# The experts' weights in a ring of eight, down weights on 96 rows, slot rows asked for on ScalarE's queue

## The reference

```python
slot = flat * C + jnp.minimum(pos, C - 1)          # C = 96 slots for each of E = 64 experts
buf = jnp.zeros((E * C, H), x.dtype).at[slot].set(x[tok]).reshape(E, C, H)
g = jnp.einsum('ech,emh->ecm', buf, Wg)            # H = 256, M = 176
u = jnp.einsum('ech,emh->ecm', buf, Wu)
out = jnp.einsum('ecm,ehm->ech', jax.nn.silu(g) * u, Wd).reshape(E * C, H)
y = jnp.sum(out[slot].reshape(T, K, H) * topk_w[..., None], axis=1)
```

## Time and profile before

| | |
|---|---|
| median of 3 runs | 1161.46 us (1160.77 to 1165.43) |
| the profiled execution | 1160.57 us |
| its span | 1158.8 us |
| TensorE busy | 1036.8 us (89%) |
| attention and shared expert | up to some 910 us |
| experts | some 910 to 1130 us |
| combine | some 1130 us to the end |

### The profile page before, as it was taken

The page is one execution under the profiler, slowest core; times in us unless marked ns, Lnnn a source line. Parts: engine busy times, 40 slices in busy tenths (PEclk is TensorE's granted clock), DMA queues, the critical chain, the costliest instruction groups (busy, mean ns, idle before and its releaser), DMA issues.

```text
span 1158.8 us, 18069 instructions
## 1 busy us (share of the span) xinstructions
PE 1036.8 (89%) x5813; PEld 859.1 (74%) x5813; DVE 613.2 (53%) x1429; ACT 493.5 (43%) x905; POOL 416.7 (36%) x601
## 2 busy tenths in 40 slices
PE   4999999999999999999999999996879887777774
PEld 4689898899989889988888899895545554444443
DVE  3674546566586567578565856853374211111116
ACT  1355555455545455554544565454220222333320
POOL 2232224432225643222763322374026143444440
PEclk9999999999999999999999999998899999999995
DMA  9960000001001100100110000002010598889866
GB/s 364 340 210 0 0 0 1 1 1 38 1 1 53 71 18 1 37 1 1 68 43 8 19 19 1 1 19 83 10 55 5 134 233 211 224 224 234 227 131 217
DMA packets 59189, 95.74 MB, mean 83 GB/s; under 512 B 8203, under 2 KB 41750, under 8 KB 58608
## 3 DMA queue, kind: packets, MB, share of 16 engines
q1 hardware_dynamic: 46880, 80.66, 21.7%
q0 software_dynamic: 12240, 14.16, 6.4%
HBM read 62.17 MB, written 42.15 MB: 90 GB/s over the span
## 4 chain that ended last, share of the span: by engine, by line
PE 72%; DMA 12%; DVE 9%; issue 3%; POOL 1%; ACT 1%; SPq 0%; DVEq 0%; POOLq 0%; ACTq 0%
PE ps L1145 21%; PE ps L1168 11%; PE ps L1192 11%; DMA wds<-in_wd 9%; PE ps L1181 9%; PE ps L1357 4%; PE ps L1229 3%; PE ps L1372 3%; PE ps L1154 2%; PE ps L1175 2%; PE ps L1157 2%; DVE arena L866 2%; PE ps L1304 2%; DMA acc<-wos,arena 1%; PE ps L1126 1%
## 5 line engine op out<-in xcount | busy, mean ns | idle before, releaser
L392 POOL TENSOR_TENSOR holdp<-neghalf 128x1 f32<-128x1 f32 x139 | 30.1, 216 | 508.7 <-DVE ss L760 267.8
L541 ACT ACTIVATE prob<-ps,rn 128x512 f32<-128x512 f32 (+3 forms) x256 | 121.1, 526 | 178.4 <-PE ps L1168 178.3
L1145 PE MATMUL ps<-wh,hth 128*128 128x384 f32 x512 | 177.8, 347 | 8.5 <-DVE wl L714 4.6
L760 DVE TENSOR_REDUCE ss<-arena 128x8 f32<-128x1024 f32 x64 | 78.1, 1220 | 198.4 <-ACT arena L525 198.3
L1145 PE MATMUL ps<-wh,htl 128*128 128x384 f32 x512 | 172.4, 337 | 0.0
L1145 PE MATMUL ps<-wl,hth 128*128 128x384 f32 x512 | 172.3, 337 | 0.0
L1168 PE MATMUL ps<-qt,kt 128*128 128x512 f32 (+3 forms) x512 | 149.6, 435 | 11.6 <-DVE arena L779 5.8
L525 ACT ACTIVATE arena<-ps 128x1024 f32<-128x1024 f32 x64 | 65.6, 1025 | 221.4 <-PE ps L1145 221.4
L1192 PEld LDWEIGHTS ps<-vx,prob 128*128 128x128 f32 x1280 | 152.9, 191 | 4.0 <-POOL prob L439 0.8
L1192 PE MATMUL ps<-vx,prob 128*128 128x129 f32 (+1 forms) x1280 | 153.4, 274 | 0.5 <-POOL prob L439 0.5
L504 POOL DMA_INDIRECT acc<-wos,arena x64 | 90.2, 1409 | 142.4 <-ACT wos L649 105.0
(11 more groups left out here) (165 smaller groups left out, 1605.1 us busy)
## 6 DMA issues: line engine op xcount, KB each, us to landing
wgus<-in_wgu SPq DMA_DIRECT2D x64, 352.0 KB
wds<-in_wd SPq DMA_DIRECT2D x64, 176.0 KB
slot_rows<-pay SPq DMA_DIRECT2D x1, 7728.0 KB, 35.5
arena<-slot_rows SPq DMA_DIRECT2D x64, 120.8 KB, 3.3
warena<-in_wqkv SPq DMA_DIRECT2D x1, 4992.0 KB, 20.2
acc<-zrow SPq DMA_DIRECT2D x2, 2048.0 KB, 30.1
warena<-acc SPq DMA_DIRECT2D x8, 512.0 KB, 7.5
wos<-in_wo SPq DMA_DIRECT2D x1, 2048.0 KB, 28.3
```

Source lines behind the costliest of these rows:

```text
L541: act_(prob[:, OFF[j]:OFF[j] + w], sflat[:, OFF[j]:OFF[j] + w], ACT.Tanh, scale=rn[:, bass.ds(head(n), 1), TT + j:TT + j + 1].squeeze(1)). ...
L760: nc.vector.tensor_reduce(ss[:].rearrange("p (c i) -> p i c", c=2), sq, X, ALU.add).then_inc(s["ss_rdy"], 1)
L1145: last = mm(ps[:, i, 0:3 * DH], hp[:, k, i * P:(i + 1) * P], wp[:, k, :], start=(k == 0 and m == 0), stop=(k == KC - 1 and m == 2))
```

## The change

It has three parts.

The down weights come from the host padded from 88 to 96 rows; the matmuls read the first 88 as before. The ring of weights has eight places: four own ones (`wge`, `wde`, loaded at the kernel's start as before) and four in tiles that the attention is through with (`prob`, `arena`, `vx`, `wos`), loaded by SyncE once the last head is done. Each weight load in the stage is then for expert u+8. The output rows keep four places (`ORING`). The load of the slot rows leaves SyncE's list; ScalarE asks for it behind `e_orow(f)`, for expert f+4, for f from 4 to 59. The wait for the scatter is the one that `e_orow` has anyway.

```diff
-RING = 4
+EARLY = 4
+RING = 8
+ORING = 4
 XR = 8
+MR = 96
@@ 
-        orow = wos[0:C, 0:RING, :]
+        orow = wos[0:C, 0:ORING, :]
+        late = XR * RW
...
+        wgus = [wge[:, u] for u in range(EARLY)]
+        wgus += [gu_place(prob[:, 0:2 * KC * M]), gu_place(prob[:, 2 * KC * M:4 * KC * M])]
+        wgus += [gu_place(arena2[:, late:late + 2 * KC * M]), gu_place(arena2[:, late + 2 * KC * M:late + 4 * KC * M])]
+        wds = [wde[:, u] for u in range(EARLY)]
+        wds += [wd_place(vx[0:MR, 1024:1536]), wd_place(vx[0:MR, 1536:2048]), wos[0:MR, 4:6, :], wos[0:MR, 6:8, :]]
@@ SyncE, after the attention
+            sp.wait_ge(s["o_rdy"], B * H)
+            sp.wait_ge(s["y_rdy"], B * H)
+            sp.wait_ge(s["x2_rdy"], 2 * B + 1)
+            for u in range(EARLY, RING):
+                sp.dma_start(wgus[u], wgu[u]).then_inc(w_in[u], 16)
+                sp.dma_start(wds[u], wd[u]).then_inc(w_in[u], 16)
@@ SyncE, in the experts
-            def rows_in(base, u):
-                sp.wait_ge(ys[u % NACC], (base + (u - RING + NACC - u % NACC)) * (16 // NACC))
-                sp.dma_start(xg[0:C, (u + RING) % XR, :], buf_d[bass.ds((base + (u + RING)) * C, C), :]).then_inc(xg_in[(u + RING) % XR], 16)
...
-                if not (first and u < RING) and not (last and u >= XR - RING):
-                    rows_in(base, u)
@@ ScalarE
+            def e_rows(e, base):
+
+                n = e + XR - ORING
+                a.dma_start(xg[0:C, n % XR, :], buf_d[bass.ds((base + n) * C, C), :]).then_inc(xg_in[n % XR], 16)
@@ 
                 e_silu(e, base)
                 if not (isinstance(base, int) and base + e < 2):
-                    e_orow(e - 2, base) if e >= 2 or isinstance(base, int) else e_orow(e - 2 + XR, base - XR)
+                    f, at = (e - 2, base) if e >= 2 or isinstance(base, int) else (e - 2 + XR, base - XR)
+                    e_orow(f, at)
+                    if not (isinstance(base, int) and not ORING <= base + f < E - (XR - ORING)):
+                        e_rows(f, at)
@@ the host
-        "wd": a("L0_ffn_Wd").transpose(0, 2, 1).reshape(E, 2, MC, D).transpose(0, 2, 1, 3),
+        "wd": np.pad(a("L0_ffn_Wd").transpose(0, 2, 1).reshape(E, 2, MC, D).transpose(0, 2, 1, 3), ((0, 0), (0, MR - MC), (0, 0), (0, 0))),
```

More of the change, by code:

```diff
@@ L86, in build @@
         gates = sb("gates", [P, KC, E])
-        wgus = sb("wgus", [P, RING, KC, 2 * M])
-        wds = sb("wds", [MC, RING, 2, D])
+        wge = sb("wge", [P, EARLY, KC, 2 * M])
+        wde = sb("wde", [MR, EARLY, 2, D])
         warena = sb("warena", [P, KC * H * 3 * DH])
@@ L191, in build, with gu_place, wd_place @@
         actt = xnf[0:MC, 512:512 + 4 * C].rearrange("p (u m c) -> p u m c", u=2, m=2)
-        orow = wos[0:C, 0:RING, :]
+        orow = wos[0:C, 0:ORING, :]
+        late = XR * RW
+        def gu_place(v):
+            return v.rearrange("p (k m) -> p k m", k=KC)
+        def wd_place(v):
+            return v.rearrange("p (m d) -> p m d", m=2)
+        wgus = [wge[:, u] for u in range(EARLY)]
[3 more added lines that the diff above has]
+        wds += [wd_place(vx[0:MR, 1024:1536]), wd_place(vx[0:MR, 1536:2048]), wos[0:MR, 4:6, :], wos[0:MR, 6:8, :]]
         accs = [warena[:, (a + 1) * NT * D:(a + 2) * NT * D].rearrange("p (i d) -> p i d", i=NT) for a in range(NACC)]
@@ L222, in build @@
         ys = [sem(f"ys{a}") for a in range(NACC)]
-        o95s = [sem(f"o95s{i}") for i in range(RING)]
+        o95s = [sem(f"o95s{i}") for i in range(ORING)]
         acc_in = [sem(f"acc_in{b}") for b in range(B)]
@@ L287, in _ @@
             sp.dma_start(gates[:], gate).then_inc(s["ld_gate"], 16)
-            for u in range(RING):
-                sp.dma_start(wgus[:, u], wgu[u]).then_inc(w_in[u], 16)
-                sp.dma_start(wds[:, u], wd[u]).then_inc(w_in[u], 16)
+            for u in range(EARLY):
+                sp.dma_start(wgus[u], wgu[u]).then_inc(w_in[u], 16)
+                sp.dma_start(wds[u], wd[u]).then_inc(w_in[u], 16)
             sp.wait_ge(s["fills"], 2)
@@ L337, in gate_up @@
                 sp.wait_ge(s["gu_ps"], base + (u + 1))
[L338 to L342 removed]
+                sp.dma_start(wgus[u % RING], wgu[bass.ds(base + (RING + u), 1)].squeeze(0)).then_inc(w_in[u % RING], 16)
             def last_row(base, u):
                 sp.wait_ge(s["orow_rdy"], base + (u + 1))
[L346 removed]
+                sp.dma_start(o95_d[bass.ds(base + u, 1)], orow[C - 1:C, u % ORING, :]).then_inc(o95s[u % ORING], 16)
             def down(base, u):
                 sp.wait_ge(s["dn_ps"], base + (u + 1))
[L350 removed]
+                sp.dma_start(wds[u % RING], wd[bass.ds(base + (RING + u), 1)].squeeze(0)).then_inc(w_in[u % RING], 16)
             def sp_period(base, u):
@@ L354, in sp_period @@
                 last = isinstance(base, int) and base == E - XR
-                if not (last and u >= XR - RING):
+                if not last:
                     gate_up(base, u)
                 if not (first and u < 2):
-                    if not (last and u - 2 >= XR - RING):
+                    if not last or u < 2:
                         down(base, u - 2)
                     last_row(base, u - 2)
-                if not (first and u < RING) and not (last and u >= XR - RING):
-                    rows_in(base, u)
             for u in range(XR):
@@ L372, in _ @@
             last_row(E - XR, XR - 1)
-            for u in range(RING):
-                sp.wait_ge(o95s[u], 16 * (E // RING))
+            for u in range(ORING):
+                sp.wait_ge(o95s[u], 16 * (E // ORING))
             sp.dma_start(o95, o95_d).then_inc(s["o95_ld"], 16)
@@ L504, in _ @@
                 pool.indirect_dma_start(acc_d[e % NACC], bass.IndirectOffsetOnAxis(ap=xg[0:C, e % XR, TOK:TOK + 1].bitcast(I32), axis=0),
-                                        orow[0:C, e % RING, :], None, bounds_check=NTOK - 1, oob_is_err=False,
+                                        orow[0:C, e % ORING, :], None, bounds_check=NTOK - 1, oob_is_err=False,
                                         compute_op=ALU.add).then_inc(ys[e % NACC], 16)
@@ L642, in e_orow @@
                 if isinstance(base, int):
-                    if e >= RING:
-                        a.wait_ge(ys[e % NACC], 16 * ((e - RING) // NACC + 1))
-                        a.wait_ge(o95s[e % RING], 16 * (e // RING))
-                else:
-                    a.wait_ge(ys[e % NACC], (base + e - RING + NACC - e % NACC) * (16 // NACC))
-                    a.wait_ge(o95s[e % RING], (base + e - e % RING) * (16 // RING))
-                act_(orow[:, e % RING, :], ps[0:C, 4 + e % 2, 0:D], ACT.Copy,
+                    if e >= ORING:
+                        a.wait_ge(ys[e % NACC], 16 * ((e - ORING) // NACC + 1))
+                        a.wait_ge(o95s[e % ORING], 16 * (e // ORING))
+                else:
+                    a.wait_ge(ys[e % NACC], (base + e - ORING + NACC - e % NACC) * (16 // NACC))
+                    a.wait_ge(o95s[e % ORING], (base + e - e % ORING) * (16 // ORING))
+                act_(orow[:, e % ORING, :], ps[0:C, 4 + e % 2, 0:D], ACT.Copy,
                      scale=xg[0:C, e % XR, bass.ds(D + (base + e), 1)]).then_inc(s["orow_rdy"], 1)
+            def e_rows(e, base):
+                n = e + XR - ORING
+                a.dma_start(xg[0:C, n % XR, :], buf_d[bass.ds((base + n) * C, C), :]).then_inc(xg_in[n % XR], 16)
             def e_period(e, base):
@@ L1356, in gu @@
                 for k in range(KC):
-                    last = mm(ps[0:C, 1 + e % 2, 0:2 * M], xgt[:, e % 2, k, :], wgus[:, e % RING, k, :], start=(k == 0), stop=(k == KC - 1))
+                    last = mm(ps[0:C, 1 + e % 2, 0:2 * M], xgt[:, e % 2, k, :], wgus[e % RING][:, k, :], start=(k == 0), stop=(k == KC - 1))
                 last.then_inc(s["gu_ps"], 1)
@@ L1371, in down @@
                 for m in range(2):
-                    last = mm(ps[0:C, 4 + e % 2, 0:D], actt[:, e % 2, m, :], wds[:, e % RING, m, :], start=(m == 0), stop=(m == 1))
+                    last = mm(ps[0:C, 4 + e % 2, 0:D], actt[:, e % 2, m, :], wds[e % RING][0:MC, m, :], start=(m == 0), stop=(m == 1))
                 last.then_inc(s["dn_ps"], 1)
```

## The result

The changed kernel takes 1418.65 us in the median (1416.56 to 1423.19, 4 runs), the kernel before 1163.45 us beside it: a ratio of 1.2184 with the interval 1.2145 to 1.2222. It is slower, as forecast, but by 255 us and not by 179; the range ended at 1390. The profiled execution took 1416.56 us with a span of 1414.8 us.

What follows compares the result with a forecast made beforehand. Before, late expert weights bound the kernel (48.9 us of waits). After, 55 passes of 6.65 us from 929.6 us reach 1295.4; 42.6 to the span's end and 1.8 outside give 1339.8, about 1341 us in the median; range 1268 to 1390.

Steps and rivals of the forecast that it cites:

- the prediction's closing balance: Whole kernel: 52 us gained where weights no longer wait, 231 lost in row waits and slow clock, 179 more.
- The place of the loss: Experts 8 to 63: the transpose behind down waits for slot rows with no lead, some 3 us each, about 170 us.
- The signs: Expert stage: granted clock 0.7 to 0.9, DMA share near 0.45, 7 to 8 scatters in 50 us.
- the pass of 6.65 us: Each pass of experts 8 to 63: 2.62 us TensorE work, 3.03 gap, 1.0 for the clock.
- The clock: TensorE after each idle 3.0 us: six of ten passes at the lower level, +1.0 us a pass.
- The wait: Down's end to next transpose: 0.10 to scaling, 0.30 to issue, 2.5 landing, 0.13 to matmul, 3.03 us.
- my light case: Slot-row landing where eight transfers were issued alone: 2.1 / 2.4 / 2.8 us; 2.5 taken as nearest to it.
- The upper bound: Slot-row landing from issue: at most 3.8 us, the full stage's median behind two weight transfers on SyncE's queue.
- The one with the clock at full: Expert passes: the clock holds, a pass of 5.65 us, 1286 us, band 1260 to 1310; chance 0.25.
- The one with the clock low in nearly all passes: Expert passes: low clock, 7.25 us, 1374 us, or rows landing as late as before, 1388; band 1366 to 1425; chance 0.20.
- The rival on the other side: Transpose behind down: rows not late, DMA engines bound the pass, kernel faster at 1144 us; chance 0.02.
- the queue rule: DMA engines take turns between queues, so rows on ScalarE's queue land as when light; standing in line costs 73 us.

Runs made afterwards that it cites:

- the twin with lead: Changed kernel with ScalarE asking for the slot rows two passes ahead, behind a wait for the scatter: 1138.4 us, ratio 0.9772.
- the 1.0034 above: Kernel before, ring of four and 88 rows, with ScalarE asking for the slot rows two passes ahead: 1165.79 us, ratio 1.0034.

## Why the prediction was right and wrong, point by point

**What bounds the kernel before: right in the main.** The weights' landing bounds it, and the ring takes those waits away. But it brings 17 us (0.9876), not the 49 of the list of waits and not the 52 written into the prediction's closing balance: the DMA engines then stand at 0.89 to 0.92 (950 to 1100 us), and the rows (29.3 us of waits in 30 passes) and the scatters become the next to be late. The balance took the pitch of TensorE, 2.5 us, for what is next; 2.9 is what the twin with lead reaches.

**The place of the loss: right.** The order showed the load behind down and the transpose right behind the same down. Undoing this part gives 0.9808, this part alone 1.2326.

**Cost of the other parts.** The four loads after the attention cost nothing visible: the first transpose of the stage starts at 911.74 us, before at 910.69, and two kernels without these loads start it at 909.0 and 913.8. The padding was put at 0 and is a small gain of its own, 6 to 7 us. What it does in the changed kernel, with the DMA engines at 0.40, no run shows.

**The size: wrong.** By the profiled execution the forecast was 1339.8 us and 1416.6 came. The transpose of expert 8 starts 2.7 us later than summed (932.34 for 929.6; 1.05 us of it are the later start of the stage, 1.70 a first wait of 4.73 in place of 3.03), the 55 passes take 1.30 us more each (7.95 for 6.65), 71.7 us, and the rest behind expert 63 takes 2.4 us more. The signs were missed on the same side: a granted clock of 0.64 where 0.7 to 0.9 was forecast, and 6 scatters in 50 us for 7 to 8. The step that failed is the pass of 6.65 us. Its mechanism was right and two of its terms were too small, the clock by 1.03 us and the wait by 0.27:
- *The clock*, put at +1.0, was about +2.0. The wait of 3.30 us leaves 7.95 - 3.30 = 4.65 us of work, against 2.62 + 1.0 = 3.62. The price of a slow pass was read from the pass at 958 us, where gate-up took 1.94 us; that pass was only partly at the lower level, and a whole one takes 2.55 for gate-up and 4.95 in all, 2.3 more than 2.62 and not 1.6. And by these numbers (4.65 - 2.62) / 2.33 = 0.87 of this price was paid in the mean, where I had taken six of ten passes. A slow pass does bring the clock back, but late: 28 of the 55 passes regain it before their end, only to lose it in the next wait, and gate-up pays in all of them.
- *The wait*, put at 3.03, was 3.30. The step from scaling to issue was 0.16, less than the 0.30 taken. The landing was 2.8, not 2.5: my light case was eight loads of rows with no weight load beside them, while here the two weight loads of the same pass are asked for just ahead; without them it is 2.1. The upper bound was misread too. The 3.8 us of the earlier trace rows is the landing of all transfers with `arena` in their name, and the scatters, which read it too, are among them; the slot rows alone took 2.3/3.3/4.1 us, so the full stage stretched them less than I had thought. That the DMA share is halved does not help if what is left stands at the same moment.
- The two are tied. At the full clock the rows follow the weights more closely and land after 3.5 us; the pass without any loss of clock is 6.6 us, not 5.65. A sum of 5.65 and a clock term hid this.

**The rivals.** The one with the clock at full did not come; made by hand, it gives 1331 us, not 1286. The one with the clock low in nearly all passes came, with 7.95 in place of the 7.25 that its top price gave for the clock alone. Its band, 1366 to 1425, held the time, but it had a chance of 0.20 and the range cut it at 1390. The rival on the other side did not come; its place, the transpose behind down, was the right one to look at, and with lead given back the time is 1138 to 1144 us against its 1144.

**What the queue rule was worth.** By the Trainium skill (DMA: Bandwidth & Descriptors, "Queues, rings and completion order") the DMA engines take turns between queues. From this the prediction took that the rows would land as in the light case. They did not: with weights beside them they landed after 2.8 us, after 3.5 at the full clock, and after 2.1 only without weights. The pairs with about equal lead and load show no saving by a queue of their own: 3.9 us against 3.3 on the shared one with the ring of four, 4.1 against 3.5 with the ring of eight and 88 rows (950 to 1100 us). The 73 us that the rule was to save rested on the misread 3.8. The advice of the Trainium skill (the same page, "Issuing engines are not separate DMA queues") that a second issuing engine saves only issue time agrees with the 1.0034 above.

## What to carry to other kernels

Count the lead of every load in passes from its issue to its first use, in the order in which both engines run; a load whose issue waits for an instruction that directly precedes its user has none, on whatever queue it stands. Its price can be more than its latency, as here, where the idle time that it made also lowered TensorE's clock for the work behind it: measure the slow pass on a stretch that is wholly slow. And read the landing time from a case with the same neighbours at the same moment, not from one with the same mean load, and for that transfer alone, not for a tile that others use too.

## What was not expected of the hardware

A few extra matmuls (three of 128 x 512 in each pass) inside a wait made the kernel 87 us faster, by keeping the granted clock at 1.00 where it was 0.64. Without lead the 121 KB of slot rows land after 2.0 to 2.1 us alone, 2.8 behind weight loads in slow passes, and 3.5 in fast ones. And with down weights that carry 16 KB of zeros per expert the kernel was faster than without them: 1155.4 us for 1162.2, and 243 for 223 GB/s over all transfers of a stretch.
